# Query products for pairs of heads, one product for values and logits, expert tiles later in the last row, and a new end

## The reference

```python
q = (x @ Wq + bq).reshape(B, S, H, DK)          # H = 16, DK = 64
k = x @ Wk + bk                                 # one key head, one value head
scores = jnp.einsum('bshd,btd->bhst', q, k) / np.sqrt(DK)
w = jax.nn.softmax(scores, axis=-1)
out = jnp.einsum('bhst,btd->bshd', w, v).reshape(B, S, H * DV) @ Wo + bo
gate_probs = jax.nn.softmax(x @ Wg + bg, axis=-1)   # 8 experts, the best two are kept
h = jax.nn.gelu(jnp.einsum('bsf,efh->bseh', x, W1) + b1)
expert_out = jnp.einsum('bseh,ehf->bsef', h, W2) + b2
```

## Time and profile before

| | |
|---|---|
| runs | 1471.53, 1472.87, 1483.64 us; median 1472.87 |
| profiled execution | 1480.48 us, span 1478.6 us |
| mean granted clock of TensorE | 0.963 of full speed |
| busy: PE, PEld | 1346.8 us (91%), 900.9 us (61%) |
| busy: DVE, ACT, POOL | 1117.6 us (76%), 694.4 us (47%), 230.4 us (16%) |
| chain that ended last | PE 58%, DVE 21%, issue 12%, POOL 5%, DMA 2% |

### The profile page before, as it was taken

The page is one execution under the profiler, slowest core; times in us unless marked ns, Lnnn a source line. Parts: engine busy times, 40 slices in busy tenths (PEclk is TensorE's granted clock), DMA queues, the critical chain, the costliest instruction groups (busy, mean ns, idle before and its releaser), DMA issues.

```text
span 1478.6 us, 18582 instructions
## 1 busy us (share of the span) xinstructions
PE 1346.8 (91%) x5393; PEld 900.9 (61%) x5393; DVE 1117.6 (76%) x2736; ACT 694.4 (47%) x1185; POOL 230.4 (16%) x283
## 2 busy tenths in 40 slices
PE   4579999999999999999999999999999699989995
PEld 2346565666666656665666666666666466767653
DVE  8786888688868886888688867886787476756582
ACT  2126454534454445444544454445444457657542
POOL 4112213100120012001200120001001042443400
PEclk9569999999999999999999999999999899999998
DMA  3402433200020003000200020000000455454152
GB/s 104 96 13 92 144 118 110 78 16 23 20 83 16 23 20 82 18 23 19 80 16 26 19 80 16 27 16 27 16 19 22 152 178 169 158 186 137 60 139 62
DMA packets 68881, 100.05 MB, mean 68 GB/s; under 512 B 25584, under 2 KB 45616, under 8 KB 64816
## 3 DMA queue, kind: packets, MB, share of 16 engines
q1 hardware_dynamic: 56400, 70.73, 15.7%
q0 software_dynamic: 10192, 27.44, 6.1%
q10 hardware_dynamic: 2192, 0.71, 0.2%
HBM read 60.14 MB, written 38.44 MB: 67 GB/s over the span
## 4 chain that ended last, share of the span: by engine, by line
PE 58%; DVE 21%; issue 12%; POOL 5%; DMA 2%; ACT 1%; SPq 1%; POOLq 0%; DVEq 0%; ACTq 0%
PE bank L1313 21%; PE bank L1293 6%; PE bank L1247 6%; PE bank L1294 6%; POOL y_rows L616 5%; DVE mneg L891 5%; PE bank L1329 4%; PE bank L1157 2%; PE bank L1159 2%; PE bank L1158 2%; DVE q_lm L885 2%; PE bank L1208 1%; PE bank L1190 1%; DVE on L1086 1%; PE bank L1198 1%
## 5 line engine op out<-in xcount | busy, mean ns | idle before, releaser
L720 ACT ACTIVATE wide<-bank 128x512 f32<-128x512 f32 x512 | 304.4, 598 | 544.9 <-PE bank L1294 503.4
L1313 PE MATMUL bank<-wide,v_w 128*128 128x512 f32 x1024 | 526.1, 596 | 0.0
L891 DVE TENSOR_REDUCE mneg<-bank 128x1 f32<-128x512 f32 x512 | 348.2, 688 | 121.7 <-PE bank L1247 97.6
L1293 PE MATMUL bank<-q_hh,k_hl 128*128 128x512 f32 x512 | 366.5, 716 | 2.1 <-ACT wide L720 1.1
L1247 PE MATMUL bank<-k_hl,q_hh 128*128 128x512 f32 x512 | 206.9, 406 | 17.1 <-DVE mneg L891 13.5
L1313 PEld LDWEIGHTS bank<-wide,v_w 128*128 128x128 f32 x1024 | 189.6, 191 | 47.2 <-issue 1.4
L597 POOL DMA_INDIRECT x_rows<-xr,slot_u x64 | 67.8, 1059 | 891.7 <-DVE slot_u L972 740.2
L1294 PE MATMUL bank<-q_lm,k_h 65*128 65x512 f32 x512 | 202.2, 395 | 0.0
L1293 PEld LDWEIGHTS bank<-q_hh,k_hl 128*128 128x128 f32 x512 | 97.4, 190 | 99.6 <-issue 93.2
L1294 PEld LDWEIGHTS bank<-q_lm,k_h 65*128 65x128 f32 x512 | 97.8, 191 | 92.8 <-issue 90.3
L885 DVE SCALAR_TENSOR_TENSOR q_lm<-bank,bq,q_hh 64x512 fp32r<-64x512 f32 x128 | 94.7, 740 | 61.9 <-ACT q_hh L669 58.1
(11 more groups left out here) (230 smaller groups left out, 1858.4 us busy)
## 6 DMA issues: line engine op xcount, KB each, us to landing
w_t<-w_rows SPq DMA_DIRECT2D x23, 1024.0 KB
x_rows<-part_h POOLq DMA_DIRECT2D x65, 258.0 KB, 4.9
inv<-inverse_scratch SPq DMA_DIRECT2D x128, 128.0 KB
w_rows<-w_t SPq DMA_DIRECT2D x8, 1024.0 KB, 4.7
x_m<-x_rows SPq DMA_DIRECT2D x23, 258.0 KB
yab<-in_L_ffn_W SPq DMA_DIRECT2D x16, 256.0 KB, 5.0
yab<-y_rows SPq DMA_DIRECT2D x8, 512.0 KB, 4.3
xin<-in_L_attn_x SPq DMA_DIRECT2D x8, 256.0 KB, 3.2
```

The lines of the kernel that those rows point to most:

```text
L720: act.activation(wide[:, st.g % WIDE, :], ps, ACT.Exp, scale=SCALE1).then_inc(wide_full, 1)
L891: dve.tensor_reduce(mneg[:, (gh // 2) % 2, col:col + 1], ps[:], X, ALU.max, negate=True)\
L1293: pe.matmul(ps, k_hl[:, n, t], q_hh[:, gh % HEADS, :], start=True, stop=False)
L1313: last = pe.matmul(ps_out[b][:], v_w[:, st.r % 2, c, :], wide[:, st.g % WIDE, :], start=(c == 0), stop=(c == TT - 1))
```

## The change

Four things change together.

The queries of two heads are made in one product: the 128 columns of weights are those of two heads instead of one head's twice. ScalarE writes the double copy now, by two activations on 64 partitions for each head, and VectorE makes both low parts one behind the other, after which the bank is free. The product is made at the last step of each even head, and six heads' queries are kept instead of four. Values and gate logits, 64 and 8 columns, come from one product of 72.

In row 7 the expert tiles stand behind steps 15, 19 and 23, with 8, 8 and 7 tiles (before: 7, 15, 19 and 23). SyncE issues the rows of the first two tiles at step 9 instead of 3. All eight yab loads stand at step 34 in buffers of their own, over the tiles' weights; before, each stood two or three steps ahead of its use.

At the end the sums of heads 12 to 15 of row 7 don't go through DRAM. VectorE inverts the 64 equal rows of sums that lie in `raw` by a reciprocal of 64x512 each, and the last projection is made in three parts, of eight, four and four heads.

```diff
-    HEADS = 4
+    HEADS = 6
...
-    INSERT = {7: 5, 15: 6, 19: 6, 23: 6}
+    INSERT = {15: 8, 19: 8, 23: 7}
...
-    LAST_AFTER = ATT + 24
+    LAST_AFTER = ATT + 6
+    DIRECT = 12
+    INVERSE_AT = {DIRECT: 58, DIRECT + 1: 62, DIRECT + 2: 65, DIRECT + 3: 67}
+    LAST_NORM_AT = {8: 60, 9: 61, 10: 63, 11: 64, 12: 64, 13: 65, 14: 66, 15: 67}
+    LAST_WO_AT = [None, ATT + 1, ATT + 4]
...
-    BEGIN_AT = {46: "xt", 48: "k", 49: "v", 50: "gl", 58: "rk"}
+    BEGIN_AT = {46: "xt", 48: "k", 49: "vg", 58: "rk"}
...
-    COMBINE_AT = [38 + 3 * n for n in range(NB)]
+    LANDED_AT = 34
+    COMBINE_AT = [39 + 3 * n for n in range(NB)]
...
-        if c == TT - 1 and 0 <= gh + LEAD + 1 < H * NB:
-            events.append(("q", gh + LEAD + 1))
+        if c == TT - 1 and h % 2 == 0 and 0 <= gh + LEAD + 1 < H * NB:
+            events.append(("q", (gh + LEAD + 1) // 2))
...
-        wq_h, wq_l = sb("wq_h", [P, H, 2, DK], F32R), sb("wq_l", [P, H, 2, DK], F32R)
+        wq_h, wq_l = sb("wq_h", [P, H // 2, P], F32R), sb("wq_l", [P, H // 2, P], F32R)
         wk_h, wk_l = sb("wk_h", [P, 2, DK], F32R), sb("wk_l", [P, 2, DK], F32R)
-        wv_h, wv_l = sb("wv_h", [P, DK], F32R), sb("wv_l", [P, DK], F32R)
-        wg_h, wg_l = sb("wg_h", [P, E], F32R), sb("wg_l", [P, E], F32R)
+        wvg_h, wvg_l = sb("wvg_h", [P, DK + E], F32R), sb("wvg_l", [P, DK + E], F32R)
...
+        inv_d = over("inv_d", [P, H - DIRECT, S], 0)
...
+        stage = nc.alloc_sbuf_tensor_at("stage", [P, 4, S], F32, offset=part_at)
...
+        yab = nc.alloc_sbuf_tensor_at("yab", [P, NB, TT, 2, P], F32, offset=tile_base)
...
+                groups = H // GROUP if r < NB - 1 else DIRECT // GROUP
+                early = r == NB - 1 and k >= 61
+                if c == 0 and 2 <= h <= GROUP * groups + 1:
...
+                if early and k in (61, 62):
+                    load_inverse(H * r + DIRECT - 2 + k - 61)
...
-                if n >= 2:
-                    sp.wait_ge(out_ready, n - 1)
-                sp.dma_start(yab[:, n % 2], y_rows[1 + 2 * S * n:1 + 2 * S * (n + 1), :]
-                             .rearrange("(i p b) d -> p i b d", p=P, b=2)).then_inc(yab_loaded[n % 2], 16)
+                sp.dma_start(yab[:, n], y_rows[1 + 2 * S * n:1 + 2 * S * (n + 1), :]
+                             .rearrange("(i p b) d -> p i b d", p=P, b=2)).then_inc(yab_loaded[n], 16)
...
-                    if st.kind == "o" and st.k == 3:
+                    if st.kind == "o" and st.k == 9:
...
-                            if st.k == COMBINE_AT[n] - (3 if n < 2 else 2):
+                            if st.k == LANDED_AT:
...
-            def round_q(gh):
-                ps, _ = filled(act, ("q", gh))
-                if gh >= HEADS:
-                    r, h = divmod(gh - HEADS, H)
+            def round_q(pair):
+                ps, _ = filled(act, ("q", pair))
+                if 2 * pair >= HEADS:
+                    r, h = divmod(2 * pair + 1 - HEADS, H)
                     act.wait_ge(first_full, g_of[r, TT * h + TT - 1] + 1)
-                act.activation(q_hh[:, gh % HEADS, :], ps[:], ACT.Identity, bias=bq[:, gh % H:gh % H + 1])\
-                   .then_inc(qh_done, 1)
+                for b in range(2):
+                    gh, rows = 2 * pair + b, slice(DK * b, DK * b + DK)
+                    for half in range(2):
+                        last = act.activation(q_hh[DK * half:DK * half + DK, gh % HEADS, :], ps[rows, :], ACT.Identity,
+                                              bias=bq[rows, gh % H:gh % H + 1])
+                    last.then_inc(qh_done, 1)
...
-            def lo_q(gh):
-                h, i = gh % H, gh % HEADS
-                dve.wait_ge(qh_done, gh + 1)
-                ps, free = full(("q", gh))
-                dve.scalar_tensor_tensor(q_lm[0:DK, i, :], ps[0:DK, :], bq[0:DK, h:h + 1],
-                                         q_hh[0:DK, i, :].bitcast(F32), ALU.add, ALU.subtract).then_inc(free, 1)
+            def lo_q(pair):
+                for b in range(2):
+                    gh, rows = 2 * pair + b, slice(DK * b, DK * b + DK)
+                    h, i = gh % H, gh % HEADS
+                    dve.wait_ge(qh_done, gh + 1)
+                    ps, free = full(("q", pair))
+                    last = dve.scalar_tensor_tensor(q_lm[0:DK, i, :], ps[rows, :], bq[rows, h:h + 1],
+                                                    q_hh[rows, i, :].bitcast(F32), ALU.add, ALU.subtract)
+                last.then_inc(free, 1)
...
+                if use == "vg":
+                    ps, free = full(("vg", n))
+                    both = ps[:, 0:TT * (DK + E)].rearrange("p (i d) -> p i d", i=TT)
+                    dve.tensor_tensor(v_w[:, i, :, 0:DK], both[:, :, 0:DK],
+                                      bv_row[:].unsqueeze(1).to_broadcast([P, TT, DK]), ALU.add)
+                    dve.tensor_tensor(gp[:], both[:, :, DK:], bg_row[:].unsqueeze(1).to_broadcast([P, TT, E]), ALU.add)\
+                       .then_inc(free, 1)
+                    read_out(dve, ("vg", n))
...
+                if r == NB - 1:
+                    for o, at_ in INVERSE_AT.items():
+                        if k == at_:
+                            gh = H * r + o
+                            emptied(dve, group_of[gh])
+                            dve.reciprocal(inv_d[0:DK, o - DIRECT, :], raw[DK:, gh % RAW, :]).then_inc(inverted_d, 1)
...
+                        if r == NB - 1 and o >= DIRECT:
+                            dve.wait_ge(inverted_d, o - DIRECT + 1)
+                            inverse = inv_d[0:DK, o - DIRECT, :]
...
-            def query(gh):
-                n, h = divmod(gh, H)
-                into(("q", gh), lambda ps: three(ps[:], twice(wq_h[:, h]), twice(wq_l[:, h]),
-                                                 x_h[:, n % 2, :], x_l[:, n % 2, :]))
+            def query(pair):
+                n, i = divmod(pair, H // 2)
+                into(("q", pair), lambda ps: three(ps[:], wq_h[:, i, :], wq_l[:, i, :], x_h[:, n % 2, :], x_l[:, n % 2, :]))
...
+            def project(r, part):
+                tiles = (slice(0, 4), slice(4, 8 if r < NB - 1 else 6), slice(6, 8))[part]
+                pe.wait_ge(normed, H * r + 2 * tiles.stop)
```

More of the change, by code:

```diff
@@ L186, in head_events, with wo_at, norm_at @@
         return events
+    def wo_at(r, part):
+        if part == 0 or r < NB - 1:
+            return WO_AT[part] if part < 2 else None
+        return LAST_WO_AT[part]
+    def norm_at(r):
+        at_ = dict(enumerate(NORM_AT))
+        if r == NB - 1:
+            at_ = {**at_, **LAST_NORM_AT}
+        return at_
     def project_events(st):
-        return [("wo", r, half) for r, k in row_steps(st) for half in range(2) if k == WO_AT[half]]
+        return [("wo", r, part) for r, k in row_steps(st) for part in range(3) if k == wo_at(r, part)]
     def l0_events(st):
@@ L304, in two_layers @@
         spare = sb("spare", [P, TILES, TT])
-        w_t = sb("w_t", [P, WT, 4, HID], F32R)
+        tile_base = nc.sbuf_base + (-nc.sbuf_base) % 64
+        sb("tile_arena", [P, WT * 4 * HID + 16])
+        w_t = nc.alloc_sbuf_tensor_at("w_t", [P, WT, 4, HID], F32R, offset=tile_base)
+        yab = nc.alloc_sbuf_tensor_at("yab", [P, NB, TT, 2, P], F32, offset=tile_base)
         b_t = sb("b_t", [P, WT, 8])
         to_f, to_u = sb("to_f", [P, TT]), sb("to_u", [P, WT, TT], U32)
-        yab = sb("yab", [P, 2, TT, 2, P])
-        stage = yab[:].rearrange("p a i b d -> p (a i b d)").rearrange("p (n s) -> p n s", s=S)
         zeros = part_h[:].rearrange("p n s -> p (n s)")[:, 0:TT * ROW].bitcast(F32)
@@ L340, in two_layers @@
         to_set, y_scattered = sem("to_set"), [sem(f"y_scattered{i}") for i in range(WT)]
-        yab_loaded = [sem(f"yab_loaded{i}") for i in range(2)]
+        yab_loaded = [sem(f"yab_loaded{i}") for i in range(NB)]
+        inverted_d = sem("inverted_d")
         resident, out_ready, stored = sem("resident"), sem("out_ready"), sem("stored")
@@ L441, in sums_and_inverses @@
                 four = r * (H // GROUP) + h // GROUP - 1
-                if c == 1 and h >= 6 and h % GROUP == 2 and h // GROUP <= H // GROUP:
+                if c == 1 and h >= 6 and h % GROUP == 2 and h // GROUP <= groups:
                     for i in range(2):
@@ L702, in _ @@
                         act.activation(wk, stage_k, ACT.Identity)
-                    act.activation(wv_h[:], stage_v, ACT.Identity)
-                    act.activation(wg_h[:], stage_g, ACT.Identity).then_inc(split_h, 1)
+                    act.activation(wvg_h[:], stage_vg, ACT.Identity).then_inc(split_h, 1)
                     for n in range(2):
                         act.wait_ge(w_q[n], 16)
-                        src = raw[:, n, :].rearrange("p (h d) -> p h d", d=DK)
-                        for hi in copies(wq_h[:, 8 * n:8 * n + 8]):
-                            last = act.activation(hi, src, ACT.Identity)
-                        last.then_inc(split_h, 1)
```

(24 more changed lines are left out.)

65 lines of the change are left out of this document (28 added, 37 removed).

## The result

The changed kernel takes 1551.37 us (median of four runs, 1547.05 to 1552.98) against 1472.2 for the kernel before beside it: a ratio of 1.0515, interval 1.0459 to 1.0572. I had forecast 1475 us, 1440 to 1493. That is 58 us above the upper end of the range.

What follows compares the result with a forecast made beforehand. TensorE was taken to set the pace in rows 0 to 6 and waits for data the last row. Terms −13 − 4 + 17 + 6 − 4 = +2 gave 1482.5 us profiled, less 7.6: 1475 us, range 1440 to 1493.

Steps and rivals of the forecast that it cites:

- What comes back: Rows, cost of pairing queries: TensorE waits behind products +9.6 us, exps delayed in steps 3 to 7 +10.5, VectorE's subtractions +11.2.
- My sign of being wrong: Wrong if TensorE loses nothing behind the products, or VectorE's waits for maxima grow by over 3 us in a row.
- Removed products: Query products: 64 of 0.70 us go, six of eight counted per row: −29.4 us for rows 0 to 6, −4.2 for row 7.
- The 72-column product: Values and logits in one product: twelve 8-column matmuls go, 1.34 us a row, −10.7 us over eight rows.
- The last row: Row 7: rows loaded later −4 us, fewer and longer groups of tiles +17, eight loads at once +6.
- The wait of 12.67 us for x_m: Step 5 of row 7: this wait goes, but an 8.9 us wait for q_lm comes at step 8: −4 us.
- 5.95 at step 40: Row 7: eight loads at once at step 34 delay the maxima row needed at step 40: +6 us, bounds −2 and +8.
- the third rival: Small transfers pass the big ones, so both new waits behind SP's loads are missing: 1459 us, chance 0.12.
- The tiles' waits for landings: Row 7, longer groups of tiles: eleven waits for landings in place of seven, +17 us, low bound +10.
- The three terms: Row 7: later load of expert rows −4 us, longer groups of tiles +17, burst of eight loads +6.
- The end: After step 58: VectorE inverts four heads itself, 3.7 us each, instead of going through DRAM: −4 us, bounds 0 and −7.
- The rival on this side: ScalarE's roundings decide, 3 us each at steps 3 and 59 of a row: +17 us, 1490 us, chance 0.17.

Runs made afterwards that it cites:

- no_copies: Changed kernel with two of ScalarE's four 64x512 roundings per pair left out (copies into the other 64 partitions): ratio 0.9965 to the kernel before.
- even_halves_first: Changed kernel with ScalarE's direct roundings first, the second head's copy a step later, VectorE waiting for the direct ones alone: ratio 1.0113 to the kernel before.
- odd_spread: Changed kernel, pair product one head later, copies from SBUF over the next two steps, VectorE waiting for direct roundings alone: ratio 0.9821 to the kernel before.
- no_pairs: Changed kernel with queries made head by head again, one 128x512 rounding and one subtraction each: ratio 0.9991 to the kernel before.
- old_last_row: Changed kernel with row 7's expert tiles, rows' load and yab loads at their old places: ratio 1.0428 to the kernel before.

## Why the prediction was wrong, by its steps

**The failed step is "What comes back", the rounding.** I priced ScalarE's additions where TensorE meets them (0.24 us behind five products, 1.5 at step 3) and VectorE's at two products and ahead of the slot (11.2 us in seven rows), 31 us in all. What happened in its place: VectorE, in order, stands for the second and the fourth rounding and makes both subtractions, and with it wait the maxima, their turning, and the one transfer, q_lm, that scores need four steps later. I looked at VectorE only in the stretches where it ended last in the trace of before, and took slack for granted everywhere else. no_copies, even_halves_first and odd_spread together show it.

In waits of TensorE per row (mean of rows 1 to 5, no_pairs and then the changed kernel) it is: for q_lm 0.1 and 3.4 us, a term that my sum doesn't have; for the maxima 3.5 and 5.1; for the slot at step 59 0.9 and 2.7. The turned scores add 0.41 at six steps. My sign of being wrong, over 3 us a row more of waiting for maxima, would not have caught this: those waits grew by 1.6, and the larger share came out at the transfer and at the slot.

Sizes inside that step: the wait of the turned scores is 0.41 us, not 0.24, and behind six of the eight products (steps 12 to 52), not five, since a 64x512 rounding adds 0.70 us behind another and not 0.59 (my upper bound 0.69; the 0.59 was from activations whose spacing didn't carry over). The step from 4 to 5 is 1.4 us longer (forecast 1.5), that from 59 to 60 2.7 in row 3 (forecast: 0.6 ahead of the slot there).

**Removed products.** I counted six of eight at 0.70 each. Even in odd_spread, where no matmul waits for a rounding, the row is only 3.0 us shorter than no_pairs' (147.7 to 144.7), not 4.2: TensorE's waits for VectorE, 5.1 us a row against 4.5, take half of the difference. With the lump in place, steps 15 to 16 and 31 to 32 are 1.36 us longer instead of 0.70 shorter.

**The 72-column product**: −1.35 us a row (forecast −1.34).

**The last row** was right in its parts, and large for the tiles. The wait of 12.67 us for x_m is gone. In these rows of the changed kernel:

```profile
1227.27 0.76 PE L1330 MATMUL bank<-q_hh,k_hl 128*128 128x512 f32 x1 [9.94 <-DMA q_lm<-mrow]
...
1465.37 6.98 SPq L515 DMA_DIRECT2D yab<-y_rows  x8
...
1478.64 0.34 SPq L466 DMA_DIRECT2D sums<-sums_scratch  x1
1479.02 0.70 SPq L445 DMA_DIRECT2D q_lm<-mrow  x1
...
1480.97 0.76 PE L1330 MATMUL bank<-q_hh,k_hl 128*128 128x512 f32 x1 [5.95 <-DMA q_lm<-mrow]
```

q_lm is 9.94 us late at step 8 (forecast 8.9) and 5.95 at step 40 (net forecast 6), so the third rival, small transfers that pass the big ones, falls. The tiles' waits for landings, idle us and times, which were 27.8 in 7:

```profile
  DMA y_rows<-y_m,to_u: 40.8, 11
```

Eleven as forecast. The four steps that held tiles before take 202.2 us with the 9.94, against 182.0: +10.3 net where I had +17, and some 12 when the three products gone from them are added back, near the low bound, for which the first waits of a group only use up slack. The three terms together are then −3 + 12 + 6 = 15 us, and old_last_row shows 13.9. Steps 32, 33, 47 and 53 are 6 to 7 us shorter than before, which I had not foreseen.

**The end.**

```profile
L1114 DVE RECIPROCAL inv_d<-raw x4: 3348/3348/3348, 1515.2 to 1534.2; 64x512 f32<-64x512 f32 x4
```

```profile
1515.79 0.80 PE L1330 MATMUL bank<-q_hh,k_hl 128*128 128x512 f32 x1
...
1538.32 3.41 PE L1367 MATMUL bank<-wo,on 128*128 128x128 f32 x16 [5.10 <-DVE on L1126]
```

A reciprocal takes 3.35 us (forecast 3.7, lower bound 3.4), 6.3 ns a column from 16 on, the slope of 22 to 32 columns in the earlier trace rows. The estimate of 4.3 us that the prediction worked out from the Trainium skill's page "VectorE: DVE Perf Modes", section "First, the fixed hardware budget", is not borne out. From step 58 to the end it is 29.3 us instead of 34.1 in the earlier trace rows: −4.8 (forecast −4).

**The rival on this side** had the right engine, ScalarE, and the wrong price: +17 us with 3 us at two steps of a row. It missed the way through VectorE to the DMA. Row 0 lost 15.7 us and the later rows 8, and the trace shows where the rest went: in row 0 the scores wait for q_lm at five steps (16, 24, 32, 48, 56), 11.7 us in all against 3.4 in a later row. With the copies left out (no_copies) 8.2 of these stay, so there VectorE's two subtractions in one piece weigh more than the lump. Why row 0 has so little slack for them is left open; in odd_spread it takes 142.8.

## What to carry to other kernels

When one product serves two consumers, add up what the second engine must now do in one piece, and follow it along the engine that reads the result in order, to the last transfer that somebody waits for: slack has to be read at that transfer, not at the first user. Then place the shared work where its first user is furthest away; here that alone was worth 4.5%, and splitting it there into pieces that fit between the loop's steps another 2.4%. At the old place, making first what VectorE waits for gave back 4.0%, while splitting the work by heads made it worse, as it held a bank longer. An engine that is busy 97% of the time, as TensorE was, can still be made to wait by a change that takes work from it.

## What the runs showed of the hardware

An activation over 64 partitions takes as long as one over 128 (683 and 687 ns with bias, 512 columns), and two or four of them back to back take 0.70 us each, where two exponentials of 128x512 took 1.09 together.

TensorE's granted clock fell after one stall of the changed row. Windows of 2 us around step 59 of row 2 (busy of PE, PEld, DVE, ACT and POOL, then granted clock, DMA share, GB/s):

```profile
568.00:570.00 2.00, 1.36 (x3) 0.30 (x2) 1.51 (x3) 1.95 (x4) 0.00 (x0) 1.00 0.00 0
570.00:572.00 2.00, 0.00 (x0) 0.00 (x0) 1.58 (x7) 1.97 (x3) 0.00 (x0) 0.95 0.00 0
572.00:574.00 2.00, 1.93 (x3) 0.90 (x4) 1.73 (x4) 0.22 (x1) 0.00 (x0) 0.50 0.00 0
574.00:576.00 2.00, 2.00 (x6) 1.08 (x5) 0.00 (x0) 1.04 (x2) 0.00 (x0) 0.69 0.00 0
```

TensorE stood still in the second window and ran at the lower level, 1.2 GHz, in the third. What this cost is seen from the first matmul behind the wait to the scores of step 61, in the changed kernel

```profile
572.07 3.54 PE L1213 MATMUL bank<-x0t,w 128*128 128x512 f32 x4 [2.65 <-DVE slot L987]
...
576.60 0.80 PE L1330 MATMUL bank<-q_hh,k_hl 128*128 128x512 f32 x1
```

and before, where the wait was shorter and the granted clock stayed at 1.00:

```profile
540.73 1.98 PE L1173 MATMUL bank<-x0t,w 128*128 128x512 f32 x4 [0.95 <-DVE slot L960]
...
543.70 0.80 PE L1293 MATMUL bank<-q_hh,k_hl 128*128 128x512 f32 x1
```

The same work takes 4.53 us in place of 2.97, so the wait of 2.65 us costs 1.6 us more than itself.
